# Two changes in one: the second layer norm taken in two halves behind the first attention, and two rests fewer between Pool's scatters

## The chip, the cores and the metric

The kernel is one launch on one core of a Trainium2 chip. The metric is the device time of one execution in microseconds (us). The core has five instruction streams that run side by side and wait for each other through semaphores: TensorE (PE), VectorE (DVE), ScalarE (ACT), GpSimd (Pool, POOL in the profile) and SyncE (SP, which issues most DMAs).

## The reference, cut to what matters

Four pairs of a mixing layer and a feed-forward layer, each added to x, which holds 64 batches of 64 tokens with 128 features:

```python
x = x + _L0_xcond_ref(_layernorm(x), ctx, ctx, tau, side, ...)   # attention 0: 16 heads over ctx
x = x + _L0_ffn_ref(_layernorm(x), g_info, W_qkv, W_proj, ...)   # attention 1: tokens in two classes, by similarity
x = x + _L1_xcond_ref(_layernorm(x), ctx, ctx, ...)              # attention 2
x = x + _L1_ffn_ref(_layernorm(x), ...)                          # routed to 8 experts, by capacity
x = x + _L2_xcond_ref(ctx, _layernorm(x), ...)
x = x + _L2_ffn_ref(_layernorm(x), ...)                          # shared expert and 8 routed ones
x = x + _L3_xcond_ref(_layernorm(x), ctx, ctx, ...)              # attention 3
x = x + _L3_ffn_ref(_layernorm(x), ...)                          # 8 experts, one for each token

def _layernorm(x, axis=-1, eps=1e-05):
    return (x - mean) / sqrt(var + eps)

def _L3_ffn_ref(x, Wr, br, W1, b1, W2, b2):
    expert_idx = argmax(x @ Wr.T + br)
    y = relu(x @ W1.T + b1) @ W2.T + b2                          # for each of 8 experts
    return y[expert_idx]
```

## The kernel before, in words

x lies in SBUF as 32 tiles of 128 tokens (`x_rows`, its first 128 columns are `X`), and most stages go over 8 chunks of 4 tiles. Each engine has its own program text (`block.vector`, `block.scalar` and so on), with a function of the same name for each stage: what one engine does in `attention`, another meets in its own `attention`. The order on an engine is the order in which the program is written; nothing is scheduled later. A helper, `pipeline`, writes a stage as a loop in hardware, `unrolled` writes it out.

**Attention.** `attention(l)` runs over 16 units of 4 batches. In turn u, PE makes the scores of unit u, turns the probabilities of unit u - 1 (L2178) and multiplies them with the values (L2192), turns the outputs of unit u - 2 (L2203) and projects them (L2214). DVE takes maxima (L994) and subtracts them (L1005), divides the outputs (L1014, L1018) and updates x (L1042); ACT takes exponentials (L1798) and moves results out of PSUM (L1837, L1805). Three turns more finish the last units. DVE also gathers the norm's statistics of each tile once x is updated (`tile_stats`, L872), three units behind. In the extra turns of the first attention DVE makes window masks and guides (`windows`, `guides`). `keep_clock` (L2077) gives PE matmuls whose result nobody reads: 5 in each extra turn, and 18 at the end of the first attention.

**The layer norm.** `norms(l)` on DVE waits for all 32 tiles' statistics and makes the variance for all tiles at once (`variance`, L909 to L915), ACT takes the root (`rstds`, L1727), DVE inverts it and refines it (`inverse_root`, L919, then `newton`, L926 to L932). The semaphores `ln_step`, `rsqrt_ready` and `norm_ready` are counted through the whole kernel; `NORM_AT[ln]` says how many such chains lie before that of norm `ln`. `norms_of(ln, ts, i)` exists already for later norms: it does the same for a part `ts` of the tiles as chain number `i` of its norm, and returns a function that does the part behind the root. `root_of` is ACT's part of it.

**The second norm and what follows.** Behind the first attention comes `prepare_own`. For each chunk ACT normalises four tiles (`normalise`, L1741), PE turns them (L2115) into psT or psY, DVE copies them to KT (L1363), PE projects the queries (L2124), DVE scales them into QT (L1367). Then `classes` sorts tokens into two classes (PE: L2561; DVE, ACT and Pool have parts) while keys and values are projected, `registers` handles five register tokens for each batch, and the second attention follows.

**The last part.** In the last attention each token's expert is found for groups of tiles: 12, 8, 4, 4 and 4 (`GROUP_TILES[1]`). When DVE has placed a group (`place`, L1235), Pool writes its rows sorted by expert to DRAM, with one indirect DMA for each tile (`scatter`, L703). The first 20 tiles are counted by `early_rows` (`EARLY_TILES` is 20); once they are there, SP reads the first sorted tiles back (L613), and 13 expert tiles of 39 are worked on while the other groups are placed. A rest (`pause`, L692) is a memset of 128x1024 elements that nobody reads, which Pool waits for. In the last part it stands behind tiles 3, 7, 11, then 13, 15, 17, 19 and so on to 31. For each expert tile DVE normalises the rows (L1593) and copies the weights (L1605), PE turns the tile (L2508) and multiplies twice (L2517, L2525), and Pool writes the result to `out` (L799).

## Time and profile before

| what | value |
|---|---|
| time, median of 3 runs | 1013.03 us (1012.9 to 1013.12) |
| time of the profiled execution | 1013.32 us |
| its span, from the first to the last instruction | 1011.5 us |
| mean granted clock of PE, as a share of the full one | 0.975 |
| PE, DVE, ACT, POOL busy | 909.9, 751.1, 578.3, 390.8 us |

The profile is of one execution. Busy time is a sum over the whole span and doesn't say what an engine waits for. In the timeline a row has start and duration in us, the engine, the line of the kernel, the operation and its tiles, the count of instructions that were merged into the row, and in brackets how long the engine was idle before it and who ended that.

### The profile page before, as it was taken

How to read it: one execution, taken by the hardware profiler on the slowest of the kernel's cores; microseconds unless marked ns; L12 is line 12 of the kernel's file. 1: busy time of each engine (PE TensorE's matmuls, PEld its weight loads, DVE VectorE, ACT ScalarE, POOL GpSimd, SP SyncE). 2: the span in 40 equal slices, each digit the busy share in tenths (PEclk: the TensorE clock that was granted, in tenths of full speed). 3: DMA queues.
4: the chain of work that ended last, by engine and by line, in shares of the span. 5: the costliest groups of instructions: out<-in, count | busy, mean ns of one | idle time of the engine just before them, and what ended most of it. 6: DMA issues, size and time to landing. Idle time of an engine off the chain costs nothing.

```text
span 1011.5 us, 32199 instructions
## 1 busy us (share of the span) xinstructions
PE 909.9 (90%) x12735; PEld 704.4 (70%) x12735; DVE 751.1 (74%) x1744; ACT 578.3 (57%) x1200; POOL 390.8 (39%) x435
## 2 busy tenths in 40 slices
PE   6899998988899998999987989989898998879897
PEld 3467885465777764788755857578854887668896
DVE  3588995556899956999789766556567999876664
ACT  4656666543566656666646763235485666433454
POOL 5234421335334211444202006735564435547554
PEclk9999999989999999999999999999999999798999
DMA  8399000000000000000099811122230111122221
GB/s 268 93 333 279 3 3 1 2 8 4 3 3 2 3 2 1 3 3 3 3 299 295 208 42 35 46 62 77 67 93 1 45 44 54 44 78 57 56 64 35
DMA packets 73695, 68.83 MB, mean 68 GB/s; under 512 B 7565, under 2 KB 68944, under 8 KB 73552
## 3 DMA queue, kind: packets, MB, share of 16 engines
q1 hardware_dynamic: 68336, 57.60, 20.4%
q0 software_dynamic: 4544, 8.94, 2.7%
q8 instruction: 103, 1.69, 0.7%
q14 instruction: 40, 0.33, 0.1%
q10 hardware_dynamic: 672, 0.27, 0.1%
HBM read 22.36 MB, written 44.67 MB: 66 GB/s over the span
## 4 chain that ended last, share of the span: by engine, by line
PE 28%; DVE 12%; issue 4%; ACT 3%; another core or an unknown queue 1%; POOL 1%; DMA 1%; DVEq 1%; POOLq 0%; SPq 0%; ACTq 0%
PE ps_sc L2517 7%; PE ps_pt L2525 4%; PE ps_sc L2452 2%; DVE work L1005 2%; PE ps_pt L2461 1%; PE ps_pt L2178 1%; PE psT L2192 1%; DVE stats L872 1%; DVE mx L994 1%; PE ps_sc L2166 1%; PE ps_pt L2093 1%; PE ps_sc L2088 1%; POOL xs_dram L703 1%; PE ps_pt L2443 1%
## 5 line engine op out<-in xcount | busy, mean ns | idle before, releaser
L1837 ACT ACTIVATE P_t<-ps_pt 128x512 f32<-128x512 f32 x256 | 140.0, 594 | 146.6 <-PE ps_pt L2178 140.2
L994 DVE TENSOR_REDUCE mx<-ps_sc 128x16 f32<-128x1024 f32 x128 | 150.2, 1215 | 19.4 <-PE ps_sc L2166 19.2
L2192 PE MATMUL psT<-VB,P_t 128*64 128x18 f32 x4096 | 145.3, 213 | 13.7 <-ACT P_t L1837 6.3
L2192 PEld LDWEIGHTS psT<-VB,P_t 128*64 128x64 f32 x4096 | 131.9, 138 | 35.6 <-ACT P_t L1837 25.8
L1005 DVE TENSOR_TENSOR work<-ps_sc,mx 128x1024 f32<-128x1024 f32 x128 | 150.1, 1214 | 0.0
L1798 ACT ACTIVATE work<-work 128x1024 f32<-128x1024 f32 x128 | 130.9, 1058 | 27.9 <-DVE work L1005 26.2
L2178 PE MATMUL ps_pt<-cst,work 128*128 128x128 f32 x1024 | 142.2, 283 | 0.0
L2178 PEld LDWEIGHTS ps_pt<-cst,work 128*128 128x128 f32 x1024 | 112.2, 143 | 26.7 <-ACT work L1798 20.6
L656 POOL TENSOR_TENSOR kbh<-KT,cst 128x512 f32<-128x512 f32 x64 | 65.3, 1042 | 134.7 <-PE ps_sc L2166 93.8
L656 POOL TENSOR_TENSOR rt<-KT,cst 128x512 f32<-128x512 f32 x64 | 65.5, 1045 | 101.5 <-PE ps_sc L2166 101.5
L2517 PE MATMUL ps_sc<-kbh,KT 128*128 128x128 f32 x624 | 89.4, 289 | 2.1 <-DVE kbh L1633 1.2
L2517 PEld LDWEIGHTS ps_sc<-kbh,KT 128*128 128x128 f32 x624 | 79.8, 200 | 6.7 <-DVE kbh L1633 3.6
L2043 ACT ACTIVATE P_t<-ps_sc,KT 128x128 f32<-128x128 f32 x156 | 44.6, 368 | 55.0 <-PE ps_sc L2517 47.8
L2525 PE MATMUL ps_pt<-VB,P_t 128*128 x468 | 68.4, 284 | 6.5 <-DVE P_t L1638 5.2
L2525 PEld LDWEIGHTS ps_pt<-VB,P_t 128*128 128x128 f32 x468 | 60.7, 198 | 8.8 <-issue 8.4
L663 POOL TENSOR_TENSOR x_rows<-x_rows,bo 128x256 f32<-128x256 f32 x64 | 43.5, 683 | 45.7 <-issue 26.4
L872 DVE BATCH_NORM_STATS2 stats<-x_rows 128x6 f32<-128x128 f32 x256 | 56.9, 280 | 4.4 <-DMA x_rows<-x_in 3.7
L703 POOL DMA_INDIRECT xs_dram<-QT,dest x32 | 31.1, 973 | 70.3 <-issue 68.3
L797 POOL DMA_INDIRECT ys_dram<-work,to_row x39 | 37.9, 973 | 39.8 <-DVE to_row L1626 19.2
L1605 DVE COPY KT<-VB 128x512 f32 (+1 forms) x78 | 34.8, 446 | 23.4 <-ACT P_t L2043 16.6
L799 POOL DMA_INDIRECT out<-work,to_row x39 | 39.0, 1000 | 34.0 <-issue 16.5
L1741 ACT ACTIVATE work<-x_rows,nmr,rstd 128x128 f32<-128x128 f32 (+1 forms) x112 | 46.8, 483 | 7.1 <-DVE nmr L932 3.0
(374 smaller groups left out, 1716.9 us busy)
## 6 DMA issues: line engine op xcount, KB each, us to landing
xs_dram<-slots SPq DMA_DIRECT2D x1, 17292.0 KB, 71.0
xs_dram<-slots SPq DMA_DIRECT2D x1, 17160.0 KB, 58.6
ctxT<-xs_dram SPq DMA_DIRECT2D x39, 65.5 KB
work<-xs_dram SPq DMA_DIRECT2D x39, 65.0 KB
VB<-L_ffn_W1b_in SPq DMA_DIRECT2D x8, 258.0 KB
ctxT<-ctxT_in SPq DMA_DIRECT2D x4, 512.0 KB, 6.9
x_rows<-x_in SPq DMA_DIRECT2D x4, 512.0 KB, 9.2
QT<-ys_dram SPq DMA_DIRECT2D x4, 512.0 KB, 6.1
```

Of the source, the lines that this page charges most:

```text
L656: pool.tensor_tensor(by_head[:, 2 * h:2 * h + 2, :, :], KT[:, at:at + 2 * S].rearrange("p (b k) -> p b k", k=S).unsqueeze(2).broadcast_to( ...
L872: v.bn_stats(stats[:, bass.ds(t, 1), :].rearrange("p o c -> p (o c)"), X[:, bass.ds(t, 1), :].rearrange("p o d -> p (o d)")).then_inc(stat ...
L994: v.tensor_reduce(mx4[:, :, HPR * t:HPR * t + HPR], sc[:, :, HPR * t:HPR * t + HPR], AX.X, ALU.max).then_inc(max_ready, 1)
L1005: v.tensor_tensor(pr[:, t], sc[:, :, g], mx4[:, :, g].unsqueeze(3).broadcast_to([128, RG, HPR, S]), ALU.subtract).then_inc(shifted, 1)
L1741: act.activation(xn[u][:, j, :], X[:, bass.ds(t, 1), :].rearrange("p o d -> p (o d)"), ACT.Identity, bias=nmr[:, bass.ds(t, 1)], scale=rst ...
L1798: act.activation(half_p, half_p, ACT.Exp).then_inc(exp_ready, 1)
L1837: act.activation(P_t[:, 512 * c:512 * c + 512], ps_pt[:, 512 * (c % 2):512 * (c % 2) + 512], ACT.Copy).then_inc(p_evac, 1)
L2043: done = act.activation(hT[s][:, cols], psS[s][:, cols], ACT.Relu, bias=w_tile[s][:, 512 + j:513 + j])
L2178: mm = pe.transpose(ps_pt[:, 512 * (c % 2) + 128 * r:512 * (c % 2) + 128 * r + 128], P_s[u % 2][:, at:at + 128], ident)
L2192: mm = pe.matmul(psT[64 * b:64 * b + 64, 144 * t + 18 * g:144 * t + 18 * g + 18], P_t[:, at:at + 64], VB[:, UNIT * u + 2 * t + b, g, :, :] ...
L2517: mm = pe.matmul(psS[r][:, 128 * b:128 * b + 128], w_tile[r][:, 128 * b:128 * b + 128], xT[r], start=True, stop=True)
L2525: mm = pe.matmul(psO[s][:, 0:128], hT[s][:, 128 * b:128 * b + 128], wv[:, bass.ds(e_back * F + (w_out_at + 128 * b), 128)], start=(b == 0) ...
```

## The change

One part concerns the second norm. Its 32 tiles are treated as two halves of 16, with a chain each, so the chains of later norms get numbers higher by one (`NORM_AT`). DVE makes the variance of the first half at the head of turn 16 of the first attention, ahead of the masks, and finishes it at the end of that turn. The second half's variance is made once the last statistics are there; DVE finishes it between its copies of chunk 0 and chunk 1. ACT takes the first root in turn 16, behind the exponential for `gcols` and a load of the table set of the root, both moved up, and the second root behind its second chunk. DVE's and ACT's stage is written out instead of looped. PE gets two waits, for the last attention outputs ahead of the first chunk and for the last update of x ahead of the second, and at the end of the attention 6 matmuls of `keep_clock` instead of 18.

The other part is the condition for a rest in the last part: it now stands behind tiles 3, 7, 11, 15, 19, and from there behind 21, 23 and so on to 31. Those behind 13 and 17 are gone.

```diff
--- before.py
+++ after.py
@@ -438,7 +438,7 @@
         KEEP_AT, BEST_AT, RANK_AT = {8: 0, 12: 1, 14: 2, 16: 3}, {9: 0, 13: 1, 15: 2, 17: 3}, {10: 0, 14: 1, 16: 2}
         PAIR_AT, PAIRS = 3, 15
         CHAIN_STEPS = 7
-        NORM_AT = [0, 1, 2, 3, 4, 6, 7]
+        NORM_AT = [0, 1, 3, 4, 5, 7, 8]
         gauss_ready = sem("gauss_ready")
         g_loaded = sem("g_loaded")
         sim_step = sem("sim_step")
@@ -702,7 +702,7 @@
                 for t in range(at + first, at + last):
                     pool.indirect_dma_start(xs_dram[m][:, :], bass.IndirectOffsetOnAxis(dest[:, t:t + 1], 0),
                                             rows_of_x[m][:, t, :], None).then_inc(early_rows if m == 1 and t < EARLY_TILES else scattered, 16)
-                    if (t % 4 == 3 and t < 28) if m == 0 else (t % 4 == 3 and t < 12 or t % 2 == 1 and t >= 12):
+                    if (t % 4 == 3 and t < 28) if m == 0 else (t % 4 == 3 and t < EARLY_TILES or t % 2 == 1 and t >= EARLY_TILES):
                         pause()
 
             pool.tensor_copy(ident8[:, :], ident[0:CHUNKS, 0:CHUNKS]).then_inc(consts_ready, 1)
@@ -1050,6 +1050,8 @@
                     v.wait_ge(reg_ready, 1)
 
                 for u in range(UNITS + 3 if l < 3 else UNITS):
+                    if l == 0 and u == UNITS:
+                        finish_first = norms_of(1, slice(0, TILES // 2), 0)
                     if u < UNITS:
                         scores(u)
                         if masked and u == 0:
@@ -1075,6 +1077,8 @@
                     if behind <= u < UNITS + behind:
                         for t in (2 * (u - behind), 2 * (u - behind) + 1):
                             tile_stats(UPD_OF[l] + 1, t)
+                    if l == 0 and u == UNITS:
+                        finish_first()
                 if l == 3:
                     four_variances(6)
                     early_shifts()
@@ -1356,18 +1360,25 @@
                 unrolled(REG_STEPS, 2, step)
 
             def prepare_own():
+                finish_second = norms_of(1, slice(TILES // 2, TILES), 1)
+
+                def take_own(k, u):
+                    v.wait_ge(xt_in_psum, CHUNKS + k + 1)
+                    v.tensor_copy(KT[:, bass.ds(k * CHUNK, CHUNK)], (psT, psY)[u][:, :]).then_inc(xt_ready, 1)
+
+                take_own(0, 0)
+                finish_second()
 
                 def step(k, turn, u, live):
-                    if live(0):
-                        v.wait_ge(xt_in_psum, CHUNKS + k + 1)
-                        v.tensor_copy(KT[:, bass.ds(k * CHUNK, CHUNK)], (psT, psY)[u][:, :]).then_inc(xt_ready, 1)
+                    if live(0) and k > 0:
+                        take_own(k, u)
                     if live(1):
                         r = (u + 1) % 2
                         v.wait_ge(q_proj, CHUNKS + k)
                         v.tensor_scalar(QT[:, bass.ds((k - 1) * CHUNK, CHUNK)], psS[r][:, :], bqkv[:, 1, 0:1],
                                         float(E) ** -0.5, ALU.add, ALU.mult).then_inc(q_ready, 1)
 
-                pipeline(v, CHUNKS, 2, 1, step)
+                unrolled(CHUNKS, 1, step)
 
             for t in range(TILES):
                 tile_stats(0, t)
@@ -1379,7 +1390,6 @@
                             bo[:, :, :].rearrange("p l d -> p (l d)"), ALU.add).then_inc(bo_ready, 1)
             prepare(0, 0, tau_s)
             attention(0)
-            norms(1)
             prepare_own()
             classes()
             registers()
@@ -1452,7 +1462,7 @@
                                             two[:, :, NE:], be[:, :].unsqueeze(1).broadcast_to([128, 2, D]),
                                             ALU.add).then_inc(y_kept, 1)
 
-                v.wait_ge(norm_ready, 2 * 3 + 2)
+                v.wait_ge(norm_ready, 2 * NORM_AT[3] + 2)
                 pipeline(v, CHUNKS, 2, 2, step)
                 routing()
 
@@ -1732,7 +1742,7 @@
 
             def normalise(ln, k, u):
 
-                if isinstance(k, int) and (k == 0 or k == 4 and ln in (4, 6)):
+                if isinstance(k, int) and (k == 0 or k == 4 and ln in (1, 4, 6)):
                     act.wait_ge(norm_ready, 2 * (NORM_AT[ln] + k // 4) + 2)
                 wait_reuse(act, xt_in_psum, CHUNKS * ln + k - 1)
                 tiles = TPC // 2 if ln in SHARED_LN else TPC
@@ -1762,7 +1772,10 @@
                 act.activation(xts[s][:, :], (psT, psY)[s][:, :], ACT.Copy).then_inc(xt_ready, 1)
 
             def prepare_own():
-                pipeline(act, CHUNKS, 2, 0, lambda k, turn, u, live: normalise(1, k, u))
+                for k in range(CHUNKS):
+                    normalise(1, k, k % 2)
+                    if k == 1:
+                        root_of(1, slice(TILES // 2, TILES), 1)
 
             def prepare(ln, last_keys, between=None):
                 def step(k, turn, u, live):
@@ -1846,8 +1859,13 @@
                         turned(u - 1)
                     elif u > UNITS:
                         outputs(u)
-                    if l == 2 and u == UNITS:
+                    if l == 0 and u == UNITS:
+                        act.wait_ge(gcol_step, 2)
+                        act.activation(gcols[:, 1, :], gcols[:, 1, :], ACT.Exp, scale=-1.0 / DEV_POW).then_inc(gauss_ready, 1)
+                    if l in (0, 2) and u == UNITS:
                         act.preload_act_table_set("sqrt_and_others")
+                    if l == 0 and u == UNITS:
+                        root_of(1, slice(0, TILES // 2), 0)
                     if u < UNITS:
                         exponentials(u)
 
@@ -1892,9 +1910,6 @@
                     rstds(0)
             prepare(0, lambda: take_all(0, CHUNKS - 1))
             attention(0)
-            act.wait_ge(gcol_step, 2)
-            act.activation(gcols[:, 1, :], gcols[:, 1, :], ACT.Exp, scale=-1.0 / DEV_POW).then_inc(gauss_ready, 1)
-            rstds(1)
             prepare_own()
             classes()
             registers()
@@ -2109,6 +2124,10 @@
                 def step(k, turn, u, live):
                     s = u % 2
                     if live(0):
+                        if l == 1 and isinstance(k, int) and k == 0:
+                            pe.wait_ge(ots_ready, UNITS)
+                        elif l == 1 and isinstance(k, int) and k == 1:
+                            pe.wait_ge(x_updated, TILES)
                         normalised(ln, k)
                         wait_reuse(pe, xt_ready, CHUNKS * ln + k - 1)
                         for j in range(TPC):
@@ -2268,7 +2287,7 @@
                         values(u - 1, 2)
                         values(u - 1, 3)
                 if l == 0:
-                    keep_clock(psS[0], 18)
+                    keep_clock(psS[0], 6)
                 elif l == 2:
                     pe.wait_ge(l2_loaded, 80)
                     keep_clock(psS[0], 4)
```

## Rows read from the trace of the kernel before

**Rows 1.** The page: the chain that ended last, by engine
```profile
PE 28%; DVE 12%; issue 4%; ACT 3%; another core or an unknown queue 1%; POOL 1%; DMA 1%; DVEq 1%; POOLq 0%; SPq 0%; ACTq 0%
```

**Rows 2.** The timeline of all engines, 153 to 164.5 us (start, duration, engine, line)
```profile
155.94 1.08 ACT L1837 ACTIVATE P_t<-ps_pt 128x512 f32<-128x512 f32 x2 [1.04 <-PE ps_pt L2178]
...
157.88 0.36 DVE L1014 RECIPROCAL rden<-psT 128x32 f32<-128x32 f32 x1 [2.82 <-PE psT L2192]
...
158.94 0.48 DVE L872 BATCH_NORM_STATS2 stats<-x_rows 128x6 f32<-128x128 f32 x2
...
159.62 0.38 ACT L1805 ACTIVATE oh<-psY 128x256 f32<-128x256 f32 x1 [2.59 <-PE psY L2203]
...
160.14 1.28 ACT L1727 ACT_TABLE_LOAD   x1
...
160.60 4.05 PE L2077 MATMUL ps_sc<-cst 128*128 128x512 bf16 x18
160.86 0.43 DVE L1042 TENSOR_TENSOR x_rows<-psY,x_rows 128x256 f32<-128x256 f32 x1 [1.44 <-issue]
...
162.10 0.22 DVE L909 TENSOR_TENSOR lnw<-stats 128x32 f32<-128x32 f32 x1
...
162.93 0.23 ACT L1727 ACTIVATE lnw<-lnw 128x32 f32<-128x32 f32 x1 [1.51 <-DVE lnw L915]
163.19 0.35 DVE L919 RECIPROCAL lnw<-lnw 128x32 f32<-128x32 f32 x1 [0.30 <-ACT lnw L1727]
```

**Rows 3.** The timeline of all engines, 164 to 184 us
```profile
164.48 7.94 ACT L1741 ACTIVATE work<-x_rows,nmr,rstd 128x128 f32<-128x128 f32 x20 [1.32 <-DVE nmr L932]
...
166.18 0.66 PE L2115 MATMUL psT<-cst,work 128*128 128x128 f32 x4 [1.53 <-ACT work L1741]
...
172.90 4.73 ACT L1741 ACTIVATE work<-x_rows,nmr,rstd 128x128 f32 x12 [0.47 <-PE psY L2115]
...
181.54 1.92 PE L2561 MATMUL ps_sc<-QT,gate 128*32 128x512 f32 x16 [0.73 <-DVE QT L1367]
```

**Rows 4.** Windows: busy us of each engine, then the granted clock
```profile
164.00:166.00 2.00, 0.65 (x4) 0.10 (x1) 0.38 (x2) 1.52 (x4) 0.00 (x0) 1.00 0.00 0
...
170.00:172.00 2.00, 2.00 (x5) 0.90 (x4) 1.17 (x2) 1.97 (x6) 1.04 (x1) 0.50 0.00 0
```

**Rows 5.** The timeline of POOL, 889 to 903 us
```profile
889.70 0.97 POOL L703 DMA_INDIRECT xs_dram<-x_rows,dest  x1 [13.11 <-DVE dest L1235]
890.97 0.96 POOL L703 DMA_INDIRECT xs_dram<-x_rows,dest  x1 [0.30 <-issue]
891.93 0.97 POOL L692 MEMSET xd<- 128x1024 f32 x1
893.18 0.97 POOL L703 DMA_INDIRECT xs_dram<-x_rows,dest  x1 [0.28 <-POOL xd L692]
...
901.40 0.96 POOL L703 DMA_INDIRECT xs_dram<-x_rows,dest  x1 [0.30 <-issue]
```

**Rows 6.** The chain that ended last, 901 to 906 us (start, duration, what)
```profile
901.40 2.39 DMA xs_dram<-x_rows,dest
...
904.33 1.83 DMA ctxT<-xs_dram
```

**Rows 7.** Timelines of POOL, ACT and DVE, 852 to 936 us
```profile
852.95 0.96 POOL L703 DMA_INDIRECT xs_dram<-x_rows,dest  x1 [0.30 <-issue]
...
854.67 1.08 ACT L1837 ACTIVATE P_t<-ps_pt 128x512 f32<-128x512 f32 x2 [3.07 <-remote]
...
892.58 1.09 ACT L1837 ACTIVATE P_t<-ps_pt 128x512 f32<-128x512 f32 x2 [2.08 <-PE ps_pt L2178]
...
906.38 0.35 DVE L1593 TENSOR_SCALAR work<-ctxT 128x128 f32<-128x128 f32 x1 [2.39 <-DMA ctxT<-xs_dram]
...
933.47 0.98 POOL L799 DMA_INDIRECT out<-work,to_row  x1 [0.30 <-issue]
...
935.29 0.29 DVE L1633 COPY kbh<-ps_sc 128x128 f32<-128x128 f32 x1 [3.63 <-remote]
```

## The prediction

> **What bounds the kernel now.** I began with the page. The chain that ended last is spread over all engines, PE at 28% and DVE at 12% as its largest named parts [rows 1]: the kernel is a string of stages, each with its own limit, and a change is worth what it takes out of the chain at its own place. So I read the timeline at the two places that the diff touches.
>
> The first is the join of the first attention and the second layer norm. From the end of the last statistics, just before 162.10, to the first normalised tile on ACT at 164.48 [rows 3] nothing runs but one short chain: five variance instructions on DVE from 162.10, the root on ACT at 162.93, and on DVE the reciprocal at 163.19 with four Newton steps behind it [rows 2]. PE spends that time on 18 matmuls that only hold its clock, 4.05 us from 160.60 [rows 2], and starts its first transposes at 166.18 [rows 3]. After that the stage is paced by ACT: 32 instructions, 7.94 us for the first 20 and 4.73 for the other 12, with a gap of 0.47 between them that ended with PE; from 164.48 to 177.63, and the class stage's matmuls begin at 181.54 [rows 3].
>
> The second is Pool's scatter of tiles 12 to 19, at the end of the last attention. Pool issues them from 889.70 with a rest after every second one, the last at 901.40 [rows 5]. The chain of waits runs through exactly these: the last scatter lands after 2.39 us, then SyncE reads the first expert tile, 1.83 [rows 6], and DVE, which sat idle for 2.39 us until then, starts the experts at 906.38 [rows 7].
>
> **The norm in two halves.** Removed: nothing of the arithmetic. The chain for tiles 0 to 15 moves ahead. Its five variance instructions (from 162.10 to just before 162.93 for 32 columns, so at most 0.8 for 16) go to DVE ahead of the window masks, around 153.3; DVE then idles for 2.82 us before 157.88 [rows 2], which hides them. Without that idle time they would cost 0.8. The masks, which end where that idle time begins (157.88 - 2.82 = 155.06), end at 155.9, and the exponential that waits for them on ACT can start only at 157.02, the end of the last copy from 155.94 [rows 2]. Behind it on ACT come this exponential (about as long as the root, 0.23), the table load of 1.28 and the root [rows 2]: 157.02 + 0.25 + 1.3 + 0.25 = 158.8. What is queued behind them on ACT is the copy of the last outputs, which began at 159.62 [rows 2], so it is not held up. On DVE the reciprocal then waits for the statistics ahead of it, which end at 158.94 + 0.48 = 159.42 [rows 2]. From the reciprocal to ACT's first tile took 164.48 - 163.19 = 1.29 with 32 columns; I take it for 16 columns too (the lower bound is nothing, the upper this 1.29). Queued behind it on DVE is the last update of x, which started at 160.86 [rows 2], when PE let it, and keeps its time. First normalised tile: 159.42 + 1.29 = 160.71 instead of 164.48: **-3.77**.
>
> The second half: DVE's statistics end before 162.10 as they did, its variance at 162.9; its root goes between ACT's second and third chunk, one instruction of at most 0.23 [rows 2] and its start: **+0.25** on the chain, since ACT paces this stage. DVE finishes this half (1.29) after copying chunk 0 and before copying chunk 1, so that copy comes about 0.7 late; PE keeps two buffers and ACT is two chunks ahead, so I charge nothing, and 0.7 if I am wrong. ACT needs it only at its fifth chunk, 3.2 us later.
>
> PE's clock matmuls fall from 18 to 6, 12 x 0.225 = 2.7 us less: they end at 161.95, just before the transposes that can start at 160.71 + 1.59 = 162.3, a chunk being four of ACT's instructions of 7.94 / 20 = 0.397 each [rows 3]. With 18 kept, PE would be in the way until 164.65. The two new waits of PE are for the last attention outputs, before 159.42, and for the last update of x, from 160.86: both are over before the tiles that it waits for anyway, so nothing. Unrolling the loops of DVE and ACT: ACT's 20 instructions ran at 0.397 each across the loop's turns, no gap to remove: nothing.
>
> The clock: PE was busy for only 0.65 of the 2.00 us from 164 to 166, and the granted clock, 1.00 there, stood at 0.50 (1.2 instead of 2.4 GHz) from 170 to 172 [rows 4]; ACT's gap of 0.47 waits for PE at the end of that [rows 3]. After the change PE's idle time ahead of the first transposes is 0.4 instead of 1.53 [rows 3]. I take it that the clock holds and the gap goes: **-0.5**; if it falls as before, 0; if it falls earlier and longer, up to +1.
>
> Sum: -3.77 + 0.25 - 0.5 = **-4.0**, between -3.5 and -2.5 if the clock falls and the late copy costs. All that follows (the classes, the register tokens, the second attention) waits for this stage on every engine, so I expect the whole shift to arrive at the end.
>
> **Fewer rests.** The rule changes for tiles 13 and 17 alone: their rests go, those after 15 and 19 stay. A scatter directly after another starts 890.97 - 889.70 = 1.27 later, one with a rest between 893.18 - 890.97 = 2.21 [rows 5]. Two rests less: 2 x 0.94 = **-1.9** at the last scatter's issue. It is on the chain [rows 6]. What else could hold the first expert tile: DVE's idle time of 2.39 before 906.38 [rows 7] is more than 1.9. The experts' steps then follow each other in DVE's fixed order up to the last slots, so the 1.9 should last.
>
> Against it speaks what consecutive scatters do to the other engines. After three in a row, the last ending at 853.91, ACT stood still until 854.67, its 3.07 us of waiting put down to no engine; after four, the last ending at 934.45, DVE stood still until 935.29, 3.63 us [rows 7]. In the stretch of the change, ACT came back at 892.58, 0.65 after the first pair ended at 891.93 [rows 5, 7]. With a series of four that pair becomes 889.70 to 894.47, and ACT may come back only at 895.1: 2.5 later. It lies beside DVE's 2.39 of idle time, of which 1.9 is now spent, so up to 2 us could come back onto the chain. Bounds for this part: -1.9 and +2.5; I take -1.9, because the work that ACT delays can itself be late by 2 us before it meets the expert tile that now comes at 904.5.
>
> The stalls look like an engine that waits for its own instructions behind the scatters' traffic. The Trainium skill, DMA: Bandwidth & Descriptors, section Queues, rings and completion order, says that instruction refills run on a queue row of their own and that each DMA engine takes turns between rows after every packet; by that rule a refill is late by a packet's time, whatever the series' length, and the sum stays -5.9. The trace speaks against it: both waits above ended only 0.8 us after their series. By the trace the sum could be -3.9.
>
> The profiled execution took 1013.32 for a span of 1011.5; the runs' median is 1013.03. 1013.32 - 4.0 - 1.9 = 1007.4; against the median, 1007.1. I say 1007.2. A measurement of this kernel can tell about 0.2%, 2 us, from no change.
>
> **Rivals.**
> (a) The longer series give back what the rests cost: stalls until the end of a series of four take ACT or DVE past the expert tile. For: the rows of 853 and 934. Against: the idle time still left. The scatter part is then between -0.5 and +2.5, the time 1008.6 to 1011.6.
> (b) The clock of PE falls in the norm stage as before or earlier, since there are 12 matmuls fewer ahead of it, and DVE's late copy adds to it: the first part is -3.5 to -2.0, the time 1007.6 to 1009.1. For: the clock did fall with 18. Against: the idle time ahead of the transposes shrinks.
> (c) The stalls fall otherwise in DVE's favour: both instruction streams get another length, and one of the waits of some 3 us (854.67, 935.29) no longer meets a series: 1004 to 1006.
> (d) Slower: one mechanism, the scatter series. Each of the two new series could hold the engine that feeds the chain for its whole length and 0.8 more, 4.8 + 0.8 = 5.6 us, where a pair cost at most about 1. Two times 4.6 is 9.2, less 1.9 and 4.0: +3.3, or 1016.4. It decides once these stalls together exceed 5.9 by over 2.
> (e) The first half doesn't come early: something queued on ACT or DVE (the load of the table, the masks) makes its root late, and it ends with the second half near 164: first part about 0, the time 1011. Against: every instruction ahead of it has slack in rows 2.
>
> **How the numbers follow.** Forecast 0.52, (a) 0.17, (b) 0.13, (c) 0.10, (d) 0.03, (e) 0.05. The forecast alone spans 1006 to 1008.5. For 8 in 10 I take in (b), most of (a), and part of (c): 1005.0 to 1010.6. Faster by over 2 us (below 1011.0): forecast, (b), (c), and most of (a), 0.91; within 2 us: the rest of (a) and (e), 0.06; slower: 0.03.
>
> **What would show it.** ACT's first L1741 instruction of this stage at about 160.7 and its last ending at 173.7, the class matmuls at about 177.5; the granted clock at 1.00 between; the root's two instructions around 158.7 and 164. At the end, seen from the first scatter of tile 12: the last one 9.8 after it instead of 11.7, the first expert tile on DVE 14.8 instead of 16.7 after it. I am wrong if ACT or DVE stands still through a series of four and DVE's idle time before the first expert tile is gone, or if the waits put down to no engine after 845 grow by as much as was saved.

## The result

| | before | after |
|---|---|---|
| time, median of 9 runs each, same chip | 1009.16 us (1006.95 to 1013.12) | 1004.21 us (1002.96 to 1011.3) |
| ratio, with its 95% interval | | 0.9952 (0.9931 to 0.9973) |
| profiled execution: its time, its span | 1013.32, 1011.5 us | 1011.3, 1009.4 us |
| mean granted clock of PE | 0.975 | 0.973 |

The kernel became faster by 4.9 us; the forecast was 5.9. The time of 1004.21 lies 0.8 us below the range, because the kernel before came out at 1009.16 in these nine runs and the forecast stood on 1013.03, the median of the first three. The profiled execution of the kernel after is the longest of its nine, so its whole span says little. What can be read is each stage against a landmark of its own.

The chain that ended last, by engine, on the page of the kernel after; it answers to [rows 1] and is spread in the same way:

```profile
PE 29%; DVE 11%; issue 3%; ACT 3%; another core or an unknown queue 1%; DMA 1%; POOL 1%; DVEq 0%; POOLq 0%; SPq 0%; ACTq 0%
```

**The norm stage.** The timelines of ACT, DVE and PE of the kernel after, which answer to [rows 2, 3]:

```profile
154.10 1.09 ACT L1850 ACTIVATE P_t<-ps_pt 128x512 f32<-128x512 f32 x2 [1.05 <-PE ps_pt L2197]
155.07 0.23 ACT L1864 ACTIVATE gcols<-gcols 128x32 f32<-128x32 f32 x1
155.32 1.28 ACT L1866 ACT_TABLE_LOAD   x1
156.61 0.22 ACT L1741 ACTIVATE lnw<-lnw 128x16 f32<-128x16 f32 x1
...
158.60 3.19 ACT L1751 ACTIVATE work<-x_rows,nmr,rstd 128x128 f32<-128x128 f32 x8 [0.44 <-DVE nmr L932]
161.69 0.20 ACT L1741 ACTIVATE lnw<-lnw 128x16 f32<-128x16 f32 x1
161.80 9.33 ACT L1751 ACTIVATE work<-x_rows,nmr,rstd 128x128 f32<-128x128 f32 x24
...
157.49 0.24 DVE L919 RECIPROCAL lnw<-lnw 128x16 f32<-128x16 f32 x1
...
158.76 1.46 PE L2092 MATMUL ps_sc<-cst 128*128 128x512 bf16 x6
160.35 0.63 PE L2134 MATMUL psT<-cst,work 128*128 128x128 f32 x4
...
174.65 1.92 PE L2580 MATMUL ps_sc<-QT,gate 128*32 128x512 f32 x16 [0.73 <-DVE QT L1378]
```

The landmark is the last pair of copies of the attention, 154.10 here and 155.94 in [rows 2]; these two executions were already 1.84 us apart there, which is none of the change's doing. From it, the first normalised tile comes 4.50 us later instead of 8.54, ACT's last one ends after 17.03 (161.80 + 9.33 - 154.10) instead of 21.69, and the class matmuls begin after 20.55 instead of 25.60. The stage is 5.05 us shorter. The granted clock, the third number from the end of a row of the windows, stays at 1.00 (2.4 GHz) where it was 0.50 in [rows 4]:

```profile
164.00:166.00 2.00, 2.00 (x10) 0.94 (x8) 1.83 (x4) 2.00 (x6) 1.10 (x2) 1.00 0.00 0
...
170.00:172.00 2.00, 2.00 (x11) 1.09 (x10) 1.83 (x4) 1.13 (x3) 1.10 (x2) 1.00 0.00 0
```

**The scatters.** Timelines of POOL, PE, ACT, DVE and SP of the kernel after, which answer to [rows 5, 7]:

```profile
884.97 0.96 POOL L703 DMA_INDIRECT xs_dram<-x_rows,dest  x1 [13.20 <-DVE dest L1239]
...
888.76 0.96 POOL L703 DMA_INDIRECT xs_dram<-x_rows,dest  x1 [0.30 <-issue]
...
894.76 0.96 POOL L703 DMA_INDIRECT xs_dram<-x_rows,dest  x1 [0.31 <-issue]
...
885.95 1.09 PE L2197 MATMUL ps_pt<-cst,work 128*128 128x128 f32 x8
...
889.24 0.60 ACT L1850 ACTIVATE P_t<-ps_pt 128x512 f32<-128x512 f32 x1 [3.46 <-remote]
...
891.32 1.05 PE L2211 MATMUL psT<-VB,P_t 128*64 128x18 f32 x16 [0.79 <-issue]
...
895.19 0.37 SPq L593 DMA_DIRECT2D VB<-L_ffn_W2T_in  x1
...
895.20 0.17 DVE L1024 CAST ei<-psT 128x8 int32<-128x8 f32 x1 [4.82 <-remote]
...
898.72 0.18 DVE L1118 CAST slot_row<-slotf 128x13 int32<-128x13 f32 x1
...
902.34 0.35 DVE L1603 TENSOR_SCALAR work<-ctxT 128x128 f32<-128x128 f32 x1 [1.12 <-DMA ctxT<-xs_dram]
```

The last scatter is issued 9.79 us after the first of tile 12 (894.76 - 884.97) instead of 11.70: the two rests are gone, exactly as priced. Yet the first expert tile starts 17.37 us after that first scatter instead of 16.68. The chain that ended last, from the last scatter on (start, duration, what), which answers to [rows 6]:

```profile
894.76 4.34 DMA xs_dram<-x_rows,dest
...
899.17 0.27 SPq L609
...
899.63 2.49 DMA ctxT<-xs_dram
```

The landing takes 4.34 us instead of 2.39 and the read 2.49 instead of 1.83, which hides a third change. DVE was idle for 4.82 us before it cast the expert numbers of the last early tiles (L1024), and so its early table of slots (L1118) was ready only at 898.90. SP reads that table at L609 before it can load the first expert tile. Had the scatter landed at once, L609 would have started at about 898.9 instead of 899.17: 0.27 us were to be had there, no more. So the gain was lost twice over, in two waits that run side by side.

**Whose standstill it is.** The profile puts the waits of 3.46 and 4.82 us down to no engine ("remote"), but the program says what they are for. ACT's copy waits for the turned probabilities (PE, L2197), of which the row ends at 887.04. DVE in front of L1024, and SP in front of its load at L593, both wait for the same attention outputs (PE, L2211), of which the row ends at 892.37; DVE starts at 895.20, SP at 895.19. The trace also has the times at which the semaphores were raised: PE's for the two halves of the turned probabilities at 889.21 and 890.65, PE's for the outputs at 895.18. Each of the three waiters starts within 0.03 us of its signal, so neither DVE nor ACT stood still of itself. All waited for TensorE, whose signals came 2.6 to 3.6 us after the ends that its rows give; the profile doesn't name an engine whose signal comes so late. The ends in PE's rows are modelled, so whether the matmuls or only their signals were late can't be read here. The two waits stand one behind the other: the late copies make PE's outputs late (they end 7.40 us after the first scatter instead of 4.67), their signal, which I call late by its distance from the row's end, is 2.81 us late on top (1.67 in the kernel before), and from that one signal come both the late table and the late loads of SP.

### The profile page after: what moved, and what is told of

It reads as the page before. It is cut to its first block and busy times, and to the rows that moved or that the text cites. A ratio compares the mean times of both kernels' runs of the same rounds, so it can differ in the third digit from the quotient of the medians.

```text
span 1009.4 us, 32096 instructions
## 1 busy us (share of the span) xinstructions
PE 908.4 (90%) x12723; PEld 703.7 (70%) x12723; DVE 751.9 (74%) x1754; ACT 577.3 (57%) x1201; POOL 388.2 (38%) x433
## 5 line engine op out<-in xcount | busy, mean ns | idle before, releaser
L2211 PE MATMUL psT<-VB,P_t 128*64 128x18 f32 x4096 | 146.8, 214 | 16.3 <-ACT P_t L1850 6.2
L2211 PEld LDWEIGHTS psT<-VB,P_t 128*64 128x64 f32 x4096 | 133.4, 139 | 38.6 <-ACT P_t L1850 26.3
L2197 PE MATMUL ps_pt<-cst,work 128*128 128x128 f32 x1024 | 144.1, 285 | 0.0
L2197 PEld LDWEIGHTS ps_pt<-cst,work 128*128 128x128 f32 x1024 | 113.8, 144 | 27.2 <-ACT work L1811 20.0
```

Source lines behind the costliest of these rows:

```text
L2197: mm = pe.transpose(ps_pt[:, 512 * (c % 2) + 128 * r:512 * (c % 2) + 128 * r + 128], P_s[u % 2][:, at:at + 128], ident)
L2211: mm = pe.matmul(psT[64 * b:64 * b + 64, 144 * t + 18 * g:144 * t + 18 * g + 18], P_t[:, at:at + 64], VB[:, UNIT * u + 2 * t + b, g, :, :] ...
```

## The experiments

The medians on A are of 9 runs each; every other one is of 6 to 12 runs beside 22 to 35 of the kernel before on the same chip. "From the first scatter" means the scatter of tile 12. The groups of runs ran on chips that I call A (the two kernels above), B (two groups), C, D and E. Which chip A is was not recorded; it may be one of the others.

| kernel | chip | median, us | ratio to before (95%) | last scatter | landing | numbers, L1024 | slot table, L1118 | first expert tile |
|---|---|---|---|---|---|---|---|---|
| before | A | 1009.16 | 1 | 11.70 | 2.39 | 6.36 | 10.75 | 16.68 |
| after | A | 1004.21 | 0.9952 (0.9931 to 0.9973) | 9.79 | 4.34 | 10.23 | 13.75 | 17.37 |
| norm part | B | 1006.07 | 0.9954 (0.9928 to 0.9979) | 11.71 | 2.27 | 6.34 | 10.76 | 16.64 |
| rests part | B | 1012.66 | 1.002 (0.9995 to 1.0045) | 9.81 | | 8.82 | 13.57 | 16.33 |
| both | B | 1007.36 | 0.9967 (0.9944 to 0.999) | 9.81 | 4.17 | 10.28 | 13.77 | 17.21 |
| norm, 18 clock matmuls | B | 1009.65 | 0.9983 (0.9955 to 1.0012) | 11.69 | 2.27 | 6.35 | 10.74 | 16.59 |
| both, bias early | C | 986.0 | 0.9924 (0.99 to 0.9947) | 9.79 | 2.45 | 5.34 | 8.77 | 14.87 |
| norm, bias late | C | 987.69 | 0.9956 (0.9934 to 0.9979) | 11.69 | 2.88 | 5.34 | 8.74 | 17.06 |
| norm, bias early | C | 988.3 | 0.995 (0.9932 to 0.9968) | 11.69 | 2.26 | 5.33 | 8.74 | 16.59 |
| norm, a rest after each | C | 990.34 | 0.9986 (0.9969 to 1.0004) | 15.46 | 2.45 | 5.34 | 11.37 | 20.49 |
| both | D | 984.39 | 0.9913 (0.9884 to 0.9942) | 9.80 | 2.31 | 5.34 | 8.79 | 14.63 |
| norm part | D | 987.92 | 0.9945 (0.9921 to 0.997) | 11.69 | 2.27 | 5.34 | 8.75 | 16.42 |
| rests part | D | 990.15 | 0.9967 (0.9948 to 0.9986) | 9.79 | 2.26 | 5.33 | 8.77 | 14.66 |
| both, bias early | D | 986.41 | 0.9935 (0.9911 to 0.9959) | 9.80 | 2.54 | 5.34 | 8.79 | 14.97 |
| both, 768 KB late | E | 1015.12 | 0.9998 (0.9967 to 1.003) | 9.79 | | 11.79 | 15.10 | 21.37 |
| norm, 768 KB late | E | 1011.81 | 0.9952 (0.9922 to 0.9983) | 11.69 | 4.82 | 6.39 | 10.74 | 19.05 |
| norm, one series of eight | E | 1014.42 | 0.9985 (0.9956 to 1.0013) | 8.85 | | 12.00 | 15.29 | 19.76 |
| both | E | 1011.37 | 0.9963 (0.9931 to 0.9995) | 9.79 | | 11.90 | 15.20 | 18.76 |
| norm, rests after 13 and 15 | B | 1010.51 | 0.9965 (0.9931 to 0.9999) | 10.76 | 3.23 | 6.39 | 9.95 | 16.53 |
| the same, bias early | B | 1011.27 | 0.9964 (0.9936 to 0.9992) | 10.75 | 2.64 | 6.42 | 9.94 | 16.00 |

The five last columns are us from the first scatter, one profile each, the three last ones to the start of the instruction, except the landing, which is from issue to landing; it is left empty where the chain of waits runs past it. The medians of the kernel before were 1012.33 (B), 991.61 (C), 992.54 (D), 1015.76 (E) and 1012.99 (B again).

### The parts apart

The norm part alone, that is the whole change with the old rule of the rests; the rests part alone is the mirror of it.

```diff
-if (t % 4 == 3 and t < 28) if m == 0 else (t % 4 == 3 and t < EARLY_TILES or t % 2 == 1 and t >= EARLY_TILES):
+if (t % 4 == 3 and t < 28) if m == 0 else (t % 4 == 3 and t < 12 or t % 2 == 1 and t >= 12):
```

> The norm in two halves alone; the rests stand as before. By the forecast's own sum this part is worth -4.0 us. By the profile of the changed kernel it is worth -5.0 (from the end of the first attention to the class matmuls that stage is 5.0 shorter), and all that the change gives: this kernel then equals the whole change or is up to 1 us faster than it. A rival holds that both parts give about -2.5 each: this kernel is then -2.5.

> The two rests fewer alone. By the forecast -1.9 us. By the theory formed on the changed kernel's profile the rows land as much later as the scatters are issued earlier (4.34 us instead of 2.39 after the last scatter), and the read of the first tile takes 2.49 instead of 1.83: between -0.5 and +1.5. In its profile the last scatter is then issued 9.8 us after the first, and the first expert tile on DVE comes 16 to 18 us after it instead of 16.7; by the forecast 14.8.

> The whole change once more, on the same chip as its parts. By both the forecast and the theory it is the sum of the two parts: -5.9 by the forecast, -5 to -3.5 by the theory.

The norm part brought 4.7 us by its ratio (0.9954), the rests part nothing (1.002), both together 3.3 (0.9967). With the new norm and 6 clock matmuls the stage takes 20.54 or 20.55 us from the landmark to the class matmuls, in every profile. In the profile of the rests part, where the old norm stands, ACT goes through all 32 tiles without a gap (timeline of ACT):

```profile
164.10 12.42 ACT L1741 ACTIVATE work<-x_rows,nmr,rstd 128x128 f32<-128x128 f32 x32 [1.32 <-DVE nmr L932]
```

and the granted clock, 0.50 in the same window of [rows 4], is 1.00 (windows):

```profile
170.00:172.00 2.00, 1.94 (x8) 0.69 (x6) 1.81 (x3) 2.00 (x6) 1.28 (x2) 1.00 0.00 0
```

There the class matmuls begin after 24.60, where the kernel before needed 25.60. So of the 5.05 us, 4.05 is the new norm (the chain taken ahead and the fewer clock matmuls together), and 1.0 is the clock, which had fallen in the profile of the kernel before and held in this one of the rests part, with the same code in that stage.

The rests part alone shows the scatter part of the story by itself: last scatter 1.9 earlier, PE's signal for the outputs 2.40 us late instead of 1.67, DVE's wait for it 3.40 us instead of 0.93, the first expert tile at 16.33 instead of 16.6 to 16.7. The whole change once more was expected at -5.9 or -5 to -3.5; it came out at -3.3.

### The clock matmuls

The norm part with 18 of them at the end of the first attention instead of 6:

```diff
                 if l == 0:
-                    keep_clock(psS[0], 6)
+                    keep_clock(psS[0], 18)
```

> The norm in two halves alone, with the 18 clock matmuls of before at the end of the first attention instead of 6. They take 12 x 0.225 = 2.7 us more, and the first transposes wait for them: if PE then only starts late and catches up on ACT, whose stage is 12.5 us long, less than 2.7 comes back; if ACT is held by PE's two buffers for that time, about 2 us. Forecast: +1.5 to +2.7 against the kernel with 6. The rival that the number of clock matmuls matters through the clock alone says no difference, or the clock falls with 6 and this kernel is the faster one.

Timelines of PE and ACT of this kernel:

```profile
158.29 4.05 PE L2092 MATMUL ps_sc<-cst 128*128 128x512 bf16 x18
162.18 0.60 PE L2134 MATMUL psT<-cst,work 128*128 128x128 f32 x4
...
162.82 9.34 ACT L1751 ACTIVATE work<-x_rows,nmr,rstd 128x128 f32<-128x128 f32 x24 [1.39 <-PE psT L2134]
```

The 18 matmuls last until 162.3, PE's first transposes stand behind them, and ACT's third chunk waits 1.39 us for PE's buffer: the class matmuls come 1.5 us later than with 6 (22.05 instead of 20.54). The cut from 18 to 6 is a part of the norm's gain, and the clock holds without them. The times agree as far as they can tell (0.9983 against 0.9954).

### The bias transfer, moved away and moved near

In the kernel after, SP issued the last load of expert weights (256 KB) at 895.19 and the load of the second bias (512 KB) at 895.61, both within a microsecond of the last scatter; in the norm part alone they had gone out some 5 us before it. First theory: these bytes make the landing late. One kernel moves the bias load ahead of the last two weight loads, in the whole change and in the norm part; another moves it behind the slot table, where it meets the last scatter though the rests are as before.

```diff
                     for e in range(NE):
+                        if e == NE - 2:
+                            sp.wait_ge(staged, 2 * units_before[4])
+                            sp.dma_start(b2_all, a["L3_ffn_b2"].broadcast_to([128, NE * D])).then_inc(b2_loaded, 16)
                         at = NE * n + 512 * e
...
-                    sp.wait_ge(staged, 2 * units_before[4])
-                    sp.dma_start(b2_all, a["L3_ffn_b2"].broadcast_to([128, NE * D])).then_inc(b2_loaded, 16)
```

> The whole change, and the 512 KB transfer of the experts' second bias issued by SP ahead of the last two loads of the experts' second weights, some 12 us before the first twenty rows' last scatter, instead of 0.9 us behind its issue. If that transfer is what made the last scatter land late (4.2 to 4.3 us against 2.3 to 2.4), the landing is 2.4 to 3.3 us (one 256 KB load is still beside it), the read behind it 1.9, and the first expert tile comes up to 1.1 us earlier after the first scatter than in the whole change (VectorE stood idle only 1.12 us before it): 16.1 to 16.5 instead of 17.2 to 17.4. If the landing is late because four scatters stand in one series, it stays at 4.2 and the tile at 17.3. In time that is 0 to -1.1 us against the whole change, small beside what these runs can tell.

> The norm part alone, with the rests as before, and the same 512 KB transfer issued some 4 us later, about when the last of the first twenty scatters is issued. If the transfer is what makes a scatter land late, its landing goes from 2.3 us to about 4.2 with the rests as they were, and the first expert tile comes 1.5 to 2.5 us later after the first scatter than in the norm part alone (18.1 to 19.1 instead of 16.6), the time 1.5 to 2.5 us up. If the series of four does it, the landing stays at 2.3 and the tile at 16.6.

> The norm part alone, with the 512 KB transfer ahead of the last two weight loads. In the norm part alone it was already out of the way (issued 4.96 us ahead of the last scatter), so both theories expect a landing of 2.3 us, the first expert tile at 16.6, and the time of the norm part alone within 0.5 us. It is the control for the transfer's new place: if the time falls, the move helps by itself.

> The norm part, with a rest behind each of the scatters of tiles 12 to 19 instead of behind every second. Four rests more at 0.94 us each: the last of the twenty is issued 14.5 to 15.5 us after the first of tile 12 instead of 11.7. If series without a rest hold ScalarE and TensorE up, the remote waits of ScalarE and VectorE among the scatters (0.4 to 0.9 us in the norm part alone, 3.5 and 4.8 in the whole change) are gone, and the last unit's outputs come earlier; if the last scatter sets the end all the same, the first expert tile comes 2.8 to 3.8 us later and the time rises by as much. If the end follows the held-up engines more than the scatters, the time is within 1 us of the norm part alone.

Chip C brought what I had not looked for: every kernel takes some 20 us less there, and no profile from it has a single wait put down to no engine, nor a signal of TensorE that is late by more than 0.4 us. The whole change with the early bias had its first expert tile at 14.87 and a ratio of 0.9924. The same 512 KB beside the last scatter made its landing 2.88 us instead of 2.26 and the tile 17.06 instead of 16.59, a quarter of what I had expected of it. And four more rests moved the last scatter by 3.8 us (15.46 instead of 11.69), the tile by 3.9 and the ratio from 0.995 to 0.9986, 3.6 us of 991.61: on this chip the first expert tile follows the last early scatter one for one, and so does the end, within intervals that are 1.8 us to either side. The two of them were expected at 14.5 to 15.5 and 2.8 to 3.8 later.

This left two explanations of chip A open, the transfer and the standstill (as I still called it), so the parts ran once more together.

> The whole change once more, beside its variant with the early bias transfer. In the runs before these, kernels were timed in two sets: in one, ScalarE and VectorE stood still for 3 to 5 us at a time through the scatter series (waits put down to no engine of this core, remote in the profile's words) and the rests' gain was gone; in the other no profile has such a wait, all kernels took some 20 us less, and the variant with the early bias got the whole 1.9 us. Theory one, the standstills eat the gain: where the profile has remote waits of 3.5 to 5 us among the scatters, the bias load is late, the last scatter lands 4.2 to 4.3 us after its issue and the first expert tile is at 17.2 to 17.4; where it has none, the bias load is early, the landing is 2.3 to 2.6 and the tile at 14.8 to 15.0, the ratio to before 0.992 to 0.9935. Theory two, four scatters in a series land late by themselves: the landing is 4.2 either way and the ratio stays at 0.995 to 0.997.

> The norm part alone once more, on the same chip as the whole change. Both theories: ratio 0.995 to 0.996, landing 2.3 us, first expert tile at 16.6. The whole change against it is what the rests are worth: theory one says 1.9 us less where no engine stands still and nothing where they do, theory two says nothing either way.

> The rests part alone once more. Theory one: ratio 0.998 (1.9 us less) with the first expert tile at 14.8 to 15.0 where no engine stands still; 1.0 to 1.002 with the tile at 16.3 to 17.4 where they do. Theory two: ratio 1.0 and a late landing either way.

> The whole change with the early 512 KB bias transfer once more. Where no engine stands still, both the whole change and this should have the tile at 14.8 to 15.0 and agree within 0.5 us. Where they stand still, the transfer is still out of the way, so the landing should be 2.4 to 3.3 us and the tile at 16.1 to 16.5, bounded by VectorE's own late work: a gain of 0.7 to 1.1 us over the whole change.

Chip D has no such wait either, and here the forecast of the scatter part comes out. The timeline of DVE of the whole change on D, first scatter at 865.79:

```profile
871.13 0.14 DVE L1024 CAST ei<-psT 128x8 int32<-128x8 f32 x1
...
874.58 0.17 DVE L1118 CAST slot_row<-slotf 128x13 int32<-128x13 f32 x1
...
880.42 0.34 DVE L1603 TENSOR_SCALAR work<-ctxT 128x128 f32<-128x128 f32 x1 [2.24 <-DMA ctxT<-xs_dram]
```

and its chain that ended last:

```profile
875.59 2.31 DMA xs_dram<-x_rows,dest
...
878.44 1.75 DMA ctxT<-xs_dram
```

The cast has no wait before it, the table is ready 0.84 us before the last scatter is even issued, that scatter lands in 2.31 and the tile starts at 14.63, 1.8 us ahead of the norm part's 16.42. The four scatters in a series do not land late by themselves. By their ratios the norm part is worth 5.5 us here (0.0055 x 992.54), the rests part 3.3, both 8.6, more than the forecast's 4.0, 1.9 and 5.9; the intervals are 2 to 3 us wide to either side and hold all three, that of the whole change only just. The early bias changed nothing where it was already early: 14.97 against 14.63, and 0.9935 against 0.9913.

### The same transfers on a chip with late signals

The last weight load and the bias load together behind the slot table, in the whole change and in the norm part:

```diff
-                        sp.dma_start(wv[:, at:at + 512].rearrange("p (j d) -> p j d", j=4),
-                                     a["L3_ffn_W2T"][e].rearrange("(j p) d -> p j d", p=128)).then_inc(experts_loaded, 16)
+                        if e < NE - 1:
+                            sp.dma_start(wv[:, at:at + 512].rearrange("p (j d) -> p j d", j=4),
+                                         a["L3_ffn_W2T"][e].rearrange("(j p) d -> p j d", p=128)).then_inc(experts_loaded, 16)
...
+                sp.wait_ge(place_step, PLACE_STEPS[1] if m == 0 else EARLY_ROWS)
+                if m == 1:
+                    sp.dma_start(wv[:, at:at + 512].rearrange("p (j d) -> p j d", j=4),
+                                 a["L3_ffn_W2T"][e].rearrange("(j p) d -> p j d", p=128)).then_inc(experts_loaded, 16)
+                    sp.dma_start(b2_all, a["L3_ffn_b2"].broadcast_to([128, NE * D])).then_inc(b2_loaded, 16)
```

> The whole change with SP's last weight load (256 KB) and the bias load (512 KB) issued together about when the last of the first twenty scatters is issued, some 4 us later than they were where no engine stands still. If these transfers make the late landing, the last scatter's landing goes from 2.3 to 3.4 to 4.3 us, the read from 1.8 to 2.5, and the first expert tile from 14.6 to 16.5 to 17.3 us after the first scatter, with the time 1.5 to 2.7 us up on the whole change. If the standstill makes it by another road, the landing stays below 2.9 us, as it was with the 512 KB alone beside it (2.88), and the tile comes only as late as VectorE's wait for the bias makes it, at most 15.5.

> The norm part alone, rests as before, and the same 768 KB at the same step. Its last scatter is issued 1.9 us later than in the whole change, so the transfers begin some 2.7 us ahead of it and should be through by the time its packets come: both theories expect a landing of 2.3 to 3.2 us and the first expert tile at 16.5 to 17.5. It shows whether the place against the scatter counts, or the transfers' being late at all.

> The norm part with no rest between the scatters of tiles 12 to 19, so eight in one series. The last of them is issued 8.9 us after the first (seven times 1.27) instead of 9.8 with one rest and 11.7 with three. Where no engine stands still, the first expert tile comes 0.9 us earlier than in the whole change, 13.7 instead of 14.6, and the time is 0.9 us less than that of the whole change. Where they do, or if the longer series makes them stand still, the bias load is late and the tile at 16 to 18.

> The whole change, base for the three others. With no remote wait in its profile: landing 2.3, first expert tile 14.6 to 15.0, ratio 0.991 to 0.9935. With remote waits of 3.5 to 5 us among the scatters: landing 4.2 to 4.3, the tile at 17.2 to 17.4, ratio 0.995 to 0.997.

Chip E has the late signals, later ones than A. In the norm part with the rests as before, the 768 KB (issued at 11.0 and 11.4, the last scatter at 11.69) gave this (chain of waits):

```profile
899.58 4.82 DMA xs_dram<-x_rows,dest
...
904.87 1.85 DMA ctxT<-xs_dram
```

A landing of 4.82 with no series of four and with DVE held for only 0.97 us: the bytes beside it are enough to make a landing late, and I had expected at most 3.2 (and the tile at 16.5 to 17.5; it came at 19.05). So I put the late landing of the kernel after down to the transfers. The norm part without the late loads was not run on E; on B, C and D it lands in 2.26 to 2.27. The loads were late in the kernel after because SP issues them behind PE's attention outputs of one unit: the rows of these end 7.40 us after the first scatter on A (4.31 on D), and SP issued the first load at 10.22, when the signal came, together with DVE's cast. In the other kernel the test failed: SP issued its two loads only at 15.4 and 15.8, since its slot table came at 15.10, and its first read stood behind them, so that the tile came at 21.37 instead of the 16.5 to 17.3 that I had expected. It shows only that the read waits for the table and for what SP issues before it.

On E the whole change says which of the two waits counts there (on A they end within 0.27 us of each other). Its chain that ended last has no landing in it:

```profile
887.50 5.19 another core or an unknown queue
...
896.01 0.19 DVE slot_row L1118
896.21 0.27 SPq L609
...
896.67 2.67 DMA ctxT<-xs_dram
```

It goes from DVE's wait of 6.49 us in front of L1024 through the slot table to SP's read. Of that wait, 2.96 us pass before the rows of PE's outputs end (8.37 after the first scatter), and the other 3.5 before their signal comes. The last scatter had been issued at 890.60, 5.6 us before the table was there. The tile came at 18.76, against 17.2 to 17.4 expected. With all eight scatters in one series the last was issued another 0.94 us earlier, the table came at 15.29 and the tile at 19.76: the rest that was saved bought nothing. I had expected 16 to 18 for such a chip. This profile also shows TensorE itself held up. The 32 matmuls of one half of the outputs, which take 1.1 us in one piece elsewhere, are torn into six groups over 5.5 us, with gaps for which PE waits for nothing that the profile shows, and DVE's wait is put down to PE by name:

```profile
893.22 1.05 PE L2211 MATMUL psT<-VB,P_t 128*64 128x18 f32 x16 [3.10 <-issue]
...
896.83 0.41 PE L2211 MATMUL psT<-VB,P_t 128*64 128x18 f32 x3 [1.03 <-issue]
...
898.80 0.17 DVE L1024 CAST ei<-psT 128x8 int32<-128x8 f32 x1 [6.58 <-PE psT L2211]
```

Its first expert tile had no wait in front of it: what held it was DVE's own late work behind the table, not the read.

### One rest less, at another place

Both versions keep the rest after tile 13 and drop only that after 17; the second also has the early bias.

```diff
-(t % 4 == 3 and t < EARLY_TILES or t % 2 == 1 and t >= EARLY_TILES)
+(t % 4 == 3 and t < 12 or t in (13, 15) or t % 2 == 1 and t >= EARLY_TILES - 1)
```

> The norm part, with the rests after tiles 13 and 15 kept and only the one after tile 17 gone, so the scatters of tiles 16 to 19 are one series. The last of the first twenty is issued 10.75 us after the first (between 11.7 and 9.8). Where the profile has remote waits: if what counts is that the first series of four holds TensorE and ScalarE up before VectorE's token numbers (its cast of the counts), these come at 6.4 us as in the norm part, the slot table at 10.8, and the first expert tile at 15.7 to 16.3, 0.3 to 0.9 us earlier than in the norm part and 1.2 or more earlier than in the whole change. If any series of four costs its gain, the numbers are late or the landing is, and the tile comes at 17 or later. Where it has none, the tile is at 15.5, the mean of the whole change and the norm part.

> The same, with the 512 KB bias load ahead of the last two weight loads. With the rest after tile 13 kept, the bias load is already issued some 4 us ahead of the last scatter, so it should not be beside its landing either way: landing 2.3 to 2.6, first expert tile within 0.3 us of the variant before. If the landing there is 2.9 or more and falls to 2.4 here, the transfer counts as well.

Chip B again, with late signals. The numbers come at 6.39, as with all rests, and the table at 9.95, 0.8 earlier than there: what holds DVE is a series of four that begins ahead of the cast, and one that begins behind it does the table no harm. It does hold PE's signals: ACT waits 3.81 us at 12.9, with a signal that is 2.40 late, where the norm part has no such wait. The tile comes at 16.53, against 15.7 to 16.3 expected and 16.64 in the norm part. What took the rest of the gain is the landing, 3.23 us instead of 2.27 (chain of waits of the first, then of the second):

```profile
893.15 3.23 DMA xs_dram<-x_rows,dest
```

```profile
900.14 2.64 DMA xs_dram<-x_rows,dest
```

With the bias load out of the way the tile comes at 16.00, the earliest on any chip with late signals. I had expected the two within 0.3 us; they are 0.5 apart. Their times (0.9965, 0.9964) can't be told from that of the norm part (0.9954) or of the whole change. No version here beats the whole change beyond the measurement on either kind of chip.

## Why the prediction missed

**The level.** The forecast was 5.9 us below 1013.03. This is the step that put the time outside the range: "against the median, 1007.1", with 1013.03 as the level. The kernel before measured 1009.16 in the nine runs, so the same difference would have been 1003.3, below the range too. The range held only what the change could do and nothing for the level, which three runs that agree within 0.22 us had made look firm. As a difference the forecast holds: 5.9 us is 0.58%, the ratio's interval runs from 0.27% to 0.69%. That it holds is in part luck, since the first part came out 1.05 us better in the profile and the second 2.6 us worse, and the interval is 4 us wide.

**First normalised tile, 4.77 us after the landmark (160.71 - 155.94): right**, measured 4.50. I had charged the 16-column chain at its upper bound of 1.29; it takes 1.11 (157.49 to 158.60).

**The second root, +0.25, and ACT's pace: a little too dear.** From ACT's first tile to its last I had 12.99 us; it took 12.53 (158.60 to 171.13), and the root's 0.20 fitted before ACT's next tile with nothing added. DVE's late copy cost nothing, as charged.

**The clock, -0.5: the mechanism was right, its size too small.** It held. Where it fell, the cost was not only ACT's gap of 0.47 but also 0.26 more on ACT's other tiles and 0.27 in the tail from the last tile to the class matmuls (3.91 us before, 3.64 in the rests part; 3.52 after), together 1.0. But it is not the change that decides this alone: the same old code kept its clock in the rests part's run on chip B and lost it again on D. The norm part: -4.0 forecast, -5.05 from profile to profile, -4.05 with the clock's luck taken out.

**The rests, -1.9: the step that failed on chip A.** It reads "I take -1.9, because the work that ACT delays can itself be late by 2 us before it meets the expert tile". The issue of the last scatter moved by 1.91 as priced. What I had not looked at is the other thing that SP's first read needs, the early slot table on DVE. It was ready 10.9 us after the first scatter, against 14.1 for the landing, 3.2 us of cover. I weighed only ACT's delay against DVE's idle time in front of the expert tile. But both engines wait for TensorE, and ACT's delay goes through TensorE's outputs on to DVE's table: the outputs' rows ended 2.7 us later than before, their signal was 1.1 us later still, DVE waited 4.82 us instead of 0.93, and the table came at 13.75. SP's loads wait for the same signal, and so 768 KB came beside the last scatter. The part came out at +0.7 in the profile (17.37 against 16.68), +0.6 on B (17.21 against 16.64). This is rival (a) in what it does to the scatter part, though the time of 1004.21 isn't the 1008.6 to 1011.6 that it named. I had given it 0.17: for it stood the rows of 853 and 934 [rows 7], and they were right. What it calls stalls of ACT or DVE are waits for TensorE's late signals. On chips C and D, without them, the forecast's 14.8 measured 14.6 to 15.0.

**The rule on queues.** By the Trainium skill, DMA: Bandwidth & Descriptors, section Queues, rings and completion order, each DMA engine takes turns between its queue rows after every packet. From that I had worked out that a refill of instructions is late by about a packet's time, whatever the length of the series. The trace speaks against refills as the cause, and so says nothing about the rule: from 886.9 to 898.9 us, while ACT and DVE waited, the profile of the kernel after has packets of the queues of SP and of Pool's scatters and none on a queue of instructions.

**The other rivals.** (b) did not happen: the clock held and the first part was better than forecast. (c) was not needed; the time it named came from the level. (d) priced each new series at 5.6 us on the chain; waits of 3.46 us on ACT and 4.82 on DVE did come, but both beside the first series. Together they moved the table by 3.0 us, of the 3.2 that it had been ahead of the landing. (e) did not happen, the first half was early by 0.27 more than forecast.

**What stays open.** Why some chips have the late signals, and whether it is the chip or something in how the program was placed on it; each kernel has one profile on a chip. And why the signal of TensorE's outputs is 2.4 to 3.5 us late behind a series of four and 1.7 us behind pairs: that an engine fetches instructions then was a guess, and the packets don't support it. The interval of the times is too wide to say how much of the 2 us between 14.6 and 16.6 arrives at the end on chips A, B and E.

## What to carry to other kernels

Before a wait on the chain is shortened, list everything else that its waiter needs, with the time at which each is ready: the difference is all that can be gained, and an engine that feeds the second one may be slowed by the very edit. When a wait is put down to no engine, look up in the program which signal it is for, and compare the waits of other engines for the same one. Put short rests between indirect scatters where TensorE's work on the way to the same waiter runs beside them, and leave them out behind it (the profiles show this in the first expert tile; the times can't tell it). Keep a large load from being issued in the same microsecond as a scatter that something waits for, and when a forecast is an absolute time, give the level its own share of the range.

## What the runs showed of the hardware

The same kernel ran in 1009 to 1016 us on three chips and in 992 on two, and what differs in the profiles is that the first have waits put down to no engine (12 to 31 us of them in all) and the others none. In each trace 1118 instructions of TensorE raise a semaphore. On A, B and E the signals of at least 55 to 65 of them come more than 0.4 us after the end of their row; on C and D not one does. Each of these late signals comes within 8 us behind the start of an indirect DMA of Pool; in the profile of the kernel after there is none from 730.6 to 845.6 us, where Pool issues no such DMA. Among the signals of DVE, ACT and Pool, counted in the same way, one in all the traces is late. The signal of one and the same outputs is 2.4 to 3.5 us late behind a series of four scatters issued every 1.27 us, and 1.7 behind pairs with a rest, which makes 2.21 us from one start to the next. A scatter lands 2.3 to 2.5 us after its issue by itself, 2.88 with 512 KB issued 1.44 us before it, 3.23 with 768 KB issued about 4 us before it, and 4.17 to 4.82 with 768 KB issued within a microsecond of it; these are single profiles, the second on chip C, the third and fourth on A, B and E. 18 matmuls that only hold PE's clock did not hold it in two of three profiles of the old norm stage, and the clock stayed full in every profile of the new one.
